# A gated cross-attention and mixture-of-experts layer on one core: the negated row maxima go through GpSimd's queue, the experts' weights in smaller pieces, and the steps around the router in another order

## What is computed

```python
x = x + tanh(g_xattn[0]) * xattn(layernorm(x), ctx, ctx, Wq, bq, Wk, bk, Wv, bv, Wo, bo)
x = x + tanh(g_ffn[0])   * ffn(layernorm(x), w_router, fc1_w, fc2_w, gate_w, up_w, down_w)

# xattn: 16 heads of 16 features, softmax over 512 keys
scores = einsum('bhqd,bhkd->bhqk', q, k) / 4;  attn = softmax(scores)
# ffn: the router picks 2 of 8 experts for each token
top_logits, top_idx = top_k(x @ w_router, 2);  weight = softmax(top_logits)
expert = (silu(proj) * gate) @ fc2_w[e]          # proj, gate = split(x @ fc1_w[e])
shared = (silu(x @ gate_w) * (x @ up_w)) @ down_w
```

## Time and profile before

| what | value |
|---|---|
| median of three runs | 477.28 us |
| the profiled execution, its own time | 477.94 us |
| span of its instructions | 476.2 us |
| TensorE busy | 463.4 us, 97% |
| VectorE busy | 338.4 us, 71% |
| ScalarE busy | 256.4 us, 54% |
| GpSimd busy | 118.8 us, 25% |

### The profile page before, as it was taken

How to read it: one execution, slowest core, us unless ns; L and a number is a source line. 1 busy time by engine, 2 the same in 40 slices (tenths; PEclk the granted TensorE clock), 3 DMA queues, 4 the chain that set the end, 5 groups by cost and what they waited for, 6 DMA issues and landing times.

```text
span 476.2 us, 8154 instructions
## 1 busy us (share of the span) xinstructions
PE 463.4 (97%) x2394; PEld 224.9 (47%) x2394; DVE 338.4 (71%) x858; ACT 256.4 (54%) x544; POOL 118.8 (25%) x143
## 2 busy tenths in 40 slices
PE   8999998999999999999999999999999999999997
PEld 7655422333222323333356564575555555555645
DVE  1888896888888898888847776655566556542574
ACT  2665475777777777777756311113566666631110
POOL 5593495000000000000001076660322333322000
PEclk9999998999999999999999999999999999999999
DMA  8679752798977222220000022232232332311931
GB/s 259 217 189 245 175 167 67 181 202 191 201 184 127 63 68 62 68 65 21 3 1 2 0 90 89 79 122 67 77 89 83 90 91 79 90 57 45 357 112 62
DMA packets 47276, 52.80 MB, mean 111 GB/s; under 512 B 8384, under 2 KB 39488, under 8 KB 47232
## 3 DMA queue, kind: packets, MB, share of 16 engines
q1 hardware_dynamic: 42432, 41.75, 33.9%
q0 software_dynamic: 3168, 8.69, 5.1%
q10 hardware_dynamic: 1632, 1.84, 1.2%
HBM read 34.52 MB, written 17.60 MB: 109 GB/s over the span
## 4 chain that ended last, share of the span: by engine, by line
PE 84%; DMA 6%; DVE 4%; SPq 3%; ACT 1%; issue 1%; POOL 1%; POOLq 0%; DVEq 0%
PE PS L1328 11%; PE PS L1240 10%; PE PS L1502 10%; PE PS L1456 10%; PE PS L1600 9%; PE PS L1510 6%; PE PS L1619 5%; PE PS L1291 4%; DMA R<-mparts 4%; PE PS L1595 3%; PE PS L1376 3%; PE PS L1614 2%; PE PS L1338 2%; PE PS L1574 2%; PE PS L1269 2%; PE PS L1582 2%
## 5 line engine op out<-in xcount | busy, mean ns | idle before, releaser
L781 DVE TENSOR_REDUCE nmax<-PS 128x1 f32<-128x512 f32 x256 | 162.4, 682 | 19.0 <-PE PS L1240 18.4
L663 ACT ACTIVATE R<-PS 128x512 f32<-128x512 f32 x256 | 133.7, 602 | 41.9 <-PE PS L1456 41.9
L1240 PE MATMUL PS<-R 96*128 96x512 bf16 x256 | 96.5, 383 | 0.8 <-DMA R<-k_parts 0.6
L1456 PE MATMUL PS<-R 98*128 98x512 bf16 x256 | 86.5, 381 | 4.4 <-DMA R<-mparts 4.0
L1328 PE MATMUL PS<-R 128*32 128x512 f32 x512 | 69.1, 612 | 0.0
L551 POOL DMA_INDIRECT token_y<-R,dest x34 | 33.0, 970 | 85.5 <-DVE R L1123 85.2
L1240 PEld LDWEIGHTS PS<-R 96*128 96x128 bf16 x256 | 24.8, 97 | 58.0 <-DVE nmax L781 38.5
L512 POOL TENSOR_TENSOR rstd<-var_eps,minus_half 128x4 f32<-128x4 f32 x4 | 4.1, 1024 | 192.6 <-DVE var_eps L764 192.5
L1600 PE MATMUL PS<-R 128*128 x100 | 47.3, 595 | 1.0 <-ACT R L737 1.0
L1456 PEld LDWEIGHTS PS<-R 98*128 98x128 bf16 x256 | 24.5, 98 | 44.1 <-ACT R L663 19.5
L682 ACT ACTIVATE R<-PS 128x512 f32<-128x512 f32 x16 | 9.6, 598 | 65.0 <-PE PS L1502 61.7
(11 more groups left out here) (173 smaller groups left out, 601.6 us busy)
## 6 DMA issues: line engine op xcount, KB each, us to landing
R<-q_parts SPq DMA_DIRECT2D x96, 64.0 KB, 3.1
R<-k_parts SPq DMA_DIRECT2D x96, 64.0 KB, 3.2
R<-in_fc_w_dram SPq DMA_DIRECT2D x8, 512.0 KB, 4.1
R<-token_y SPq DMA_DIRECT2D x4, 1024.0 KB, 10.1
R<-slot_x SPq DMA_DIRECT2D x25, 129.0 KB, 2.1
k_parts<-R SPq DMA_DIRECT2D x8, 384.0 KB, 3.3
q_parts<-R SPq DMA_DIRECT2D x8, 384.0 KB, 2.8
fc<-in_fc_w_dram SPq DMA_DIRECT2D x8, 256.0 KB, 5.0
```

Of the source, the lines that this page charges most:

```text
L663: nc.scalar.activation(PT[:, kt, j, :], PS[:, (G * (TB * i + kt) + j) % 3, :], ACT.Exp).then_inc(exp_done, 1)
L781: nc.vector.tensor_reduce(nmax[:, i % 2, j * TB + qt:j * TB + qt + 1], PS[:, smax_bank(n), :], AX.X, ALU.max, negate=True).then_inc(max_re ...
L1240: mm(PS[:, smax_bank(n), :], QS[g][0:KS, j, qt * P:(qt + 1) * P], KST[g][0:KS, j, :], start=True, stop=True).then_inc(smax_done, 1)
L1456: mm(PS[:, n % 3, :], KST[g][0:KM, j, kt * P:(kt + 1) * P], QS[g][0:KM, j, :], start=True, stop=True).then_inc(st_done, 1)
```

## The change

**Queues.** `load_max` moves from SyncE to GpSimd for groups 1 to 15; group 0's stays on SyncE as `load_first_max` with a semaphore of its own. GpSimd's 16 additions to `X`, which stood in one block, are put in fours behind the copies of groups 1 to 4.

**Loads.** `load_group(3)` is issued before `store_parts(3)` instead of behind it. The experts' weights go one expert a pass, in passes 2 to 9 (0.75 MB each), instead of two a pass in passes 2 to 5; the clearing of spare rows moves to pass 10. With `load_max` gone from the loop, the weights of a pass stand right behind that pass's `load_group`.

**Order around the router.** `gate_up` is cut in its `wgate` and `wup` halves (`gate_or_up`), and `router(2)`, `rank(2)`, `h2_transpose(3)`, `router(3)`, `router_rows(3)` and `count` stand at other places between them; VectorE's steps follow. `USERS` and `gu_bank` change accordingly.

```diff
@@ SyncE
-            def load_max(i):
+            def load_first_max():
                 for part, s in ((0, m1_ready), (1, m2_ready)):
-                    sp.wait_ge(s, i + 1)
-                    sp.dma_start(QS[i % NG][KS + part:KS + part + 1, :, :].rearrange("p h n -> p (h n)"),
-                                 mparts[:, i % 2, part, :]).then_inc(m_in[i % 2], 16)
+                    sp.wait_ge(s, 1)
+                    sp.dma_start(QS[0][KS + part:KS + part + 1, :, :].rearrange("p h n -> p (h n)"),
+                                 mparts[:, 0, part, :]).then_inc(first_m_in, 16)
...
-            load_max(0)
+            load_first_max()
+            load_group(3)
             store_parts(3)
...
             for i in range(GROUPS):
-                if i + 3 < GROUPS:
+                if 0 < i and i + 3 < GROUPS:
                     load_group(i + 3)
-                if i + 1 < GROUPS:
-                    load_max(i + 1)
-
...
-                if 2 <= i < 2 + E // 2:
-                    e = slice(2 * (i - 2), 2 * (i - 1))
+                if 2 <= i < 2 + E:
+                    e = slice(i - 2, i - 1)
...
-                if i == 2 + E // 2:
+                if i == 2 + E:
@@ GpSimd
-            pool.wait_ge(tg_bo_ready, 1)
-            for t in range(NT):
-                nc.gpsimd.tensor_tensor(X[:, t, :], X[:, t, :], tg_bo[:, :], ALU.add).then_inc(x_biased, 1)
+            def load_max(i):
+                for part, s in ((0, m1_ready), (1, m2_ready)):
+                    pool.wait_ge(s, i + 1)
+                    nc.gpsimd.dma_start(QS[i % NG][KS + part:KS + part + 1, :, :].rearrange("p h n -> p (h n)"),
+                                        mparts[:, i % 2, part, :]).then_inc(m_in[i % 2], 16)
+
+            load_max(1)
+            for i in range(2, GROUPS):
+                if i < 2 + B:
+                    pool.wait_ge(tg_bo_ready, 1)
+                    for t in range((i - 2) * TB, (i - 1) * TB):
+                        nc.gpsimd.tensor_tensor(X[:, t, :], X[:, t, :], tg_bo[:, :], ALU.add).then_inc(x_biased, 1)
+                load_max(i)
@@ TensorE
             h2_transpose(2)
-            gate_up(0, 2)
+            gate_or_up(0, 2, 0)
             router(2)
+            gate_or_up(0, 2, 1)
+            router_rows(2)
             gate_up(0, 3)
-            router_rows(2)
+            rank(2)
+            gate_or_up(1, 0, 0)
             h2_transpose(3)
-            gate_up(1, 0)
-            rank(2)
+            gate_or_up(1, 0, 1)
             router(3)
+            gate_up(1, 1)
             router_rows(3)
-            gate_up(1, 1)
+            gate_up(1, 2)
             rank(3)
-            gate_up(1, 2)
-            count()
             down(0)
             gate_up(1, 3)
```

More of the change, by code:

```diff
@@ L280, in gu_bank, with max_loaded @@
                 return k
-            return (2, 6)[k] if n < IC else 2 + k
+            return (2, 6)[k] if n < IC + 2 else 2 + k
         def down_bank(b, t):
             return 6 + t // 2 if b < B - 1 else 4 + t
+        def max_loaded(eng, i):
+            if i:
+                eng.wait_ge(m_in[i % 2], 32 * ((i + 1) // 2))
+            else:
+                eng.wait_ge(first_m_in, 32)
         def qk_bank(b, j):
@@ L1085, in _ @@
             residual(3)
+            h2t_second(2)
             statistics(3)
-            h2t_second(2)
-            normalised(3)
             logits_turned(2)
-            hidden(0, 2)
             logits(2)
             choose(2)
+            hidden(0, 2)
+            normalised(3)
+            place(2)
+            hidden(0, 3)
             h2t_second(3)
-            hidden(0, 3)
-            place(2)
             logits_turned(3)
@@ L1100, in _ @@
             nc.vector.tensor_tensor(sc[:, 0, :], mx8[:, :, 1], mx8[:, :, 0], ALU.subtract).then_inc(gap_ready, 1)
+            hidden(1, 1)
             place(3)
-            hidden(1, 1)
+            hidden(1, 2)
             tabulate()
-            hidden(1, 2)
             for h in range(2):
@@ L1483, in _, with gate_or_up @@
             out_transpose(GROUPS - 1)
-            def gate_up(b, c):
[L1487 to L1504, removed]
+            def gate_or_up(b, c, k):
+                n = IC * b + c
+                if k == 0:
+                    if n == 0:
+                        pe.wait_ge(w_in["shared"], 48)
+                        pe.wait_ge(exp_done, G * TB * GROUPS)
+                    if n == 1:
+                        pe.wait_ge(ot_ready, GROUPS)
+                    if n == IC + 3:
+                        pe.wait_ge(lg_ready, B)
+                    if c == 0:
+                        for d in range(DC):
+                            pe.wait_ge(h2t_ready[d], b + 1)
+                    if n >= 2:
+                        pe.wait_ge(hs_ready, n - 1)
+                w = (wgate, wup)[k]
+                for d in range(DC):
+                    last = mm(PS[:, gu_bank(n, k), :], w[:, d, c * P:(c + 1) * P], H2T[:, d, b * S:(b + 1) * S],
+                              start=(d == 0), stop=(d == DC - 1))
+                if k == 1:
+                    last.then_inc(gu_done, 1)
+            def gate_up(b, c):
+                gate_or_up(b, c, 0)
+                gate_or_up(b, c, 1)
             def down_part(b, c, t):
@@ L1519, in down @@
                         pe.wait_ge(ctx_ready, GROUPS)
+                        pe.wait_ge(hs_ready, IC + 2)
+                    if b == 0 and c == 1:
+                        count()
                     for t in range(TB - (open_parts if c == IC - 1 else 0)):
```

14 lines of the change are left out of this document (7 added, 7 removed).

## The result

| | before | after |
|---|---|---|
| median of 7 runs each, us | 476.99 (475.88 to 477.98) | 475.06 (474.06 to 475.88) |
| ratio, 95% interval | | 0.9947 [0.9923, 0.997] |
| profiled execution, us | 477.94 | 475.06 |
| its span, us | 476.2 | 473.3 |

The forecast said 3.3 us slower. The change made the kernel 0.5% faster: 1.9 us by the medians, 2.9 us between the two profiled executions.

A forecast was written before the change was run, and what follows sets the result against it. TensorE, busy 97% of the span, bounds the kernel, so time comes from its waits. Gains 3.98 + 2.9 + 1.0 = 7.9 us against 14 x 0.8 = 11.2 us give +3.3 on 477.28: 480.6 us, range 470.5 to 489.

The forecast's parts named there:

- L = 0.8 us: Lateness of a group's start behind the 3.39 us after its maxima's transposition; 0.8 us in groups 1 to 14, 11.2 us.
- the rhythm of 12.8 us a group: Sign in the later profile: marks that end attention groups come 12.8 us apart, against 11.96 before.
- the 14 alike waits: Sign in the later profile: TensorE waits for the copied maxima alike in groups 1 to 14, about L - 0.2 us each.
- Rival B: Lateness about 0.4 to 0.7 us, or quick GpSimd but loads slowing copies; gains cancel, 475 to 479.7 us; chance 0.21.
- Rival A: GpSimd copies as quick as SyncE's, L up to 0.1; whole 7.9 us gained, 469.4 us; most of the 0.32 for faster.
- Group 1, 3.98 us: Attention group 1: early `load_group(3)` removes 2.39 us of late start and 1.59 us of half-speed products.
- Groups 3 to 10, 2.9 us: Attention groups 3 to 10: one expert's weights a pass instead of two removes the 2.9 us lost there.
- Order around the router, -1.0 us: Around the router: TensorE's waits of 0.74 us for `LT` and 0.36 us for the logits go; -1.0 us (0 to -1.5).
- the 0.2 us at `down(0)`: New wait at `down(0)` for `hidden(1, 1)`, which VectorE does behind `choose(3)`: 0.1 to 0.2 us.
- Rivals C and D: GpSimd copies slow as indirect transfers, 491.8 us; or VectorE holding GpSimd back, 490.4 us; chance 0.15 together.
- rival E: Spread loads quiet nothing: 1 to 1.5 us of the 2.9 us in groups 3 to 10 remain; no chance of its own.
- The chance for faster, 0.32: Chance given to the change making the kernel faster, most of it near GpSimd being as quick as SyncE.

The follow-up runs named there:

- experiments 7 and 8: Changed kernel, shared weights moved to passes 10 to 12, one or two awaited GpSimd clearings between the copies of groups 2 to 14: 0.9913 with one, 0.9942 with two.
- experiment 3: Kernel before with only the copies of groups 1 to 15 moved to GpSimd's queue; loads, weights and order stay: 481.81 us, ratio 1.0055.
- 5: Changed kernel with the copies issued by SyncE behind the pass's loads and weights: ratio 0.9883 to the kernel before, on a slower chip.
- experiment 6: Kernel before with only `load_group(3)` moved ahead of `store_parts(3)`: ratio 0.9969.
- experiment 9: Changed kernel with the experts' weights two experts a pass again (passes 2 to 5): 479.71 us, ratio 1.005 to the kernel before.
- experiment 4: Kernel before with only the new order around the router: 476.98 us, ratio 0.9989.

## Why the prediction was wrong

**The term that failed: L = 0.8 us for the copies on GpSimd, 11.2 us in the sum.** It was taken as the middle between SyncE's behaviour and the indirect transfers of the earlier trace rows, on the reason that "the delay and the spacing come from the engine and its queue". They don't: in the changed kernel the indirect transfers still take 0.96 us each (955 to 1113 ns), and the direct ones on the same engine 0.50. A direct transfer starts 0.29 us behind its result, not 0.78, is spaced 0.50 us and not 1.26, and lands in 1.5 us and not 2.4. L is 0, the lower bound. The prediction had named this as the point at which its sign would fall: a spacing under 0.8 and a start at once. The sentence set apart from the sum, the 2.0 us in all of the Trainium skill, "DMA: Bandwidth & Descriptors", section "Anatomy of one DMA", gave the right L; by the trace it is 1.8 us, 0.29 from the result to the issue and 1.5 from there to the landing. The later first byte for GpSimd that its section "Latency and other measured facts" states (about 1 us against 0.6) does not show in the landing: 1.5 us here, 1.7 on SyncE's queue.

The range, 470.5 to 489.0, held the time. (Its lower end, at L = 0.1, is 470.8 by the forecast's own sum.) Of the signs named ahead, the rhythm of 12.8 us a group and the 14 alike waits did not come (11.96, and none but one), the clock stayed up at group 1 but not at group 2, and of the waits of `router_rows` 0.2 us are left.

**The price of a lateness was right.** In experiments 7 and 8 a copy that lands up to 0.5 us too late makes the group late by the same time, at full clock. A whole 0.8 us was not tried, but behind waits of 1.17 to 1.42 us the clock was full too (experiments 3, 5 and 6). So the rule by which the sum went from L to the time holds as far as it was tested; the size of L was wrong.

**The term that was missing: the weights now pass the copy, 3.8 us at group 2.** I costed the queue that the copies enter and not the one they leave. In SyncE's list, `load_max(i + 1)` stood between the group's loads and the pass's weights and held the weights back until the maxima were there. With the copies gone, pass 1's 1.5 MB goes out 4 us ahead of group 2's copies and is in flight with them. Rival B named it, with a quick GpSimd and loads "reaching closer to the maxima", and the measured time stands at the lower end of its 475 to 479.7 us; but it had no term for it, and its main case was a slow GpSimd. Rival A's 7.9 us less this term is 4.1 us, against 2.9 measured, or 3.6 without the 0.7 us by which attention began later.

**Group 1, 3.98 us: came, as 3.77.** The reason was half right. I gave it to the late issue at 70.20, and there it was most of the lateness; but experiment 3 issued at once and waited 2.50 us still, since beside the same loads the copies then took 3.7 to 4.0 us to land. The loads of group 3 are the cause either way, so the edit that cures most of it is the earlier `load_group(3)` (2.6 us alone, experiment 6); the other queue adds the last 1.1 us, since it doesn't stand behind the wait for the stores.

**Groups 3 to 10, 2.9 us: came, as 2.82, for the right reason**, the DMA share falling from 0.93 to 0.44. But the spread's worth depends on the order: 4.9 us where the weights go ahead of the copy (experiment 9).

**Order around the router, -1.0 us: -0.84 in the middle.** Both waits of the earlier trace rows went, the 0.2 us at `down(0)` came as reckoned, and the first slot moved by 0.84 us. Alone it gave 0.35 us and no measurable difference. In all kernels with the new order and the copies on SyncE the middle took 85.1 us, with GpSimd 84.7; the other 0.4 us comes with the copies' queue, and by what path is open.

**Rivals C and D** were excluded by the first row: the copies took 484 to 777 ns in all 30 cases, with VectorE busy 10.7 of 12 us beside them; nothing held GpSimd back for a whole reduction. Of rival E nothing is left. The chance for faster, 0.32, was too small by the weight I gave to GpSimd's indirect rows.

## What to carry to other kernels

When a waiting transfer moves from one queue to another, cost both queues: what it will stand behind on the new one, and what it no longer holds back on the old one. A small copy on the critical path needs a quiet moment more than a queue of its own; put bulk loads behind it, or spread them so thin that they are over before it. And where a group has 0.5 us of slack, a copy's price is zero up to there and full beyond it, so a forecast must say on which side of the slack the price lies.

## What the runs showed of the hardware

- A direct transfer on GpSimd's queue: start 0.29 us behind its result, 0.50 us each, landing 1.5 us. Only its first one was slower, 0.78 us.
- The same 4 KB copy lands in 1.5 us when the DMA engines are quiet (3% busy from 97.0 to 99.1 us) and in 3.0 to 4.1 us when the shared weights keep them 94% busy around its issue; on SyncE's queue, behind the same weights, 2.6 to 3.5 us. A queue of its own gave it no precedence.
- After TensorE's idle times of 1.17, 1.18, 1.35 and 1.42 us the next products ran at full clock; after 1.60, 2.01, 2.07, 2.22, 2.50 and 2.53 us eight of them took 1.9 us instead of 1.06 (after 2.28 us, in experiment 4, 1.5 us), and the group lost 1.5 to 1.8 us on top of the idle time, against at most 0.2 behind the shorter ones.
